# The first group of a fused FFN: order of ScalarE's, VectorE's and SyncE's work at the start

## The chip, the cores and the metric

One core of a Trainium2 chip runs the whole program. Its engines are TensorE (PE), ScalarE (ACT), VectorE (DVE), GpSimd (POOL) and SyncE (SP, which issues the loads). The metric is the device time of one execution in microseconds. TensorE's clock has two levels, 1.2 and 2.4 GHz; the profile gives the granted one as 0.50 and 1.00.

## The reference

Tokens: 2 x 2048 rows of 256 numbers. The program computes a gated FFN with routing, causal attention, and the same FFN again:

```python
x = x + 0.5 * _L0_ffn_ref(_layernorm(x), ...)
x = x + _L0_attn_ref(_layernorm(x), Wq, Wk, Wv, Wo)
x = x + 0.5 * _L0_ffn_ref(_layernorm(x), ...)

# _L0_ffn_ref, the part that the start computes
xln = _ln(x, ln1_w, ln1_b)
att_out = sigmoid(xln @ Wr) * (xln @ Wv) @ Wo
rwkv_state = xln @ Ws                     # used as rwkv_state @ W2
x = x + att_out
h = _ln(x, ln2_w, ln2_b)                  # bids, routing, three experts
```

## The kernel before

Every float32 product is made of three fp32r products: each operand is split in a part hi (the value rounded) and a part lo (value minus hi), and hi*hi, hi*lo, lo*hi are summed. The splits of weights are made once at the start from the raw weights, with the layer norm's weight multiplied in: w_hi by ACT (`split_hi`, L376 and L374), w_lo by DVE (`split_lo`, L384). `early_plan` lists them in order: four for Wr and Wv (RV = 4), then W1, Wo, W3 and the bid columns up to RVS = 10, then two for the product Ws W2 up to EARLY = 12.

The FFN's first part works on 8 groups of 512 rows (NG = 8, four tiles of 128 rows each). For a group g, in order:

- DVE: statistics of the rows (`row_stats`: four bn_stats at L805, four aggregates at L809); POOL: two reciprocal roots of them (`rs1`, L746 to L751, by a power operation at L749)
- ACT: z = normalized rows (`normalize`, L583); PE: z transposed in PSUM (`transpose_z`, L411); ACT: zT_hi (`z_hi`, L619); DVE: zT_lo (`lo`, L824)
- PE: six chains `U(g, n)` of six 512-wide matmuls each (L393): r, v, r, v, then two for the state; a chain needs zT_lo, and from the fourth on the gates that free its bank: n=3 waits for the first sigmoid
- ACT: sigmoid of r (`sig_r`, L632, needs the bias columns); DVE: times v (`gv`, L829); ACT gT_hi (L638), DVE gT_lo (`g_lo`, L835); PE: `Wo(g)`, 24 matmuls of 256
- ACT: y (L598, the doubly normalized rows), s_gate (`sig_s`, L644); DVE: y + Wo's result (L842), then statistics and the second half of the FFN for the groups before

Each engine's queue is written out by hand in a loop over k, in which group k, k-1 and k-2 are in different stages. The waits between engines are semaphores.

At the start there is extra work. PE: `setup_first`, eight one-column products (each 2 matmuls of 128x1; here four columns) of raw_w with the layer norm's bias (L355); `setup_states`, the product of Ws and W2 (L523); `setup_rest`, more one-column products. ACT, in this order: z of group 0, w_hi of Wr and Wv, zT_hi, the other w_hi, the copy of the states' product (L673) and its w_hi, z of group 1, and then the first sigmoid. DVE: statistics of group 0, four w_lo, the bias copy (L932), zT_lo, statistics of group 1, the other w_lo. In later groups row_stats waits for POOL's rs1 of the group before it, ahead of its bn_stats. SP: x0, ln, ident, raw_w (1 MB), raw_w_st (776 KB), x1, five small tables, x2, x3.

Of the kernel before, what the change touches and what calls it, by code (L numbers as in the profile page):

```python
# [62 lines left out]
def build_kernel(nc, x, w256, w_st, k_w, v_w, w_qkv, ln, shares, ident, tri, mask, tok, slot_row, out):  # L63
    with ExitStack() as ctx:
# [258 lines left out]

def setup_sync(sp, b, s, f, xg, given):
    ln, ident, w256, w_st, tri, mask, shares, tok, slot_row = given
    sp.dma_start(b.x[0][:], xg[0]).then_inc(f["x_in"][0], 16)
    sp.dma_start(b.ln[:], ln).then_inc(s.first, 16)
    sp.dma_start(b.ident[:], ident).then_inc(s.first, 16)
    sp.dma_start(b.raw_w[:].rearrange("p m c n -> p (m c n)"), w256).then_inc(s.w, 16)
    sp.dma_start(b.raw_st[:], w_st).then_inc(s.st, 16)  # L330
    sp.dma_start(b.x[1][:], xg[1]).then_inc(f["x_in"][1], 16)
    for to, given in ((b.trif, tri), (b.maskf, mask), (b.shares, shares), (b.tok, tok), (b.slot_row, slot_row)):
        sp.dma_start(to[:], given).then_inc(s.const, 16)
    for g in range(2, X_BUFS):
        sp.dma_start(b.x[g][:], xg[g]).then_inc(f["x_in"][g], 16)
# [40 lines left out]
            act.mul(hi, raw, scale).then_inc(done, 1)  # L376


def split_lo(dve, plan, first, end, ready, done):

    for n in range(first, end):
        raw, scale, hi, lo = plan[n]
        dve.wait_ge(ready, n + 1)
        dve.scalar_tensor_tensor(lo, raw, 1.0 if scale is None else scale, hi.bitcast(F32), ALU.mult,  # L384
                                 ALU.subtract).then_inc(done, 1)

# [28 lines left out]
def ffn_a_tensor(pe, b, f, s, a=None):  # L415

    def U(g, first, end):
        for n, (m, fc) in enumerate(((0, 0), (1, 0), (0, 1), (1, 1), (2, 0), (2, 1))):
            if not first <= n < end:
                continue  # L420
            if n == 0:
                pe.wait_ge(f["zlo"], 2 * g + 2)
                if g >= 2:
                    pe.wait_ge(f["bd"], g - 1)
            if n < 3 and g == 1:
                pe.wait_ge(f["gv"], 2)
# [109 lines left out]

    if s:
        setup_first()
        transpose_z(pe, b, f, 0)
        setup_states()  # L540
    else:
        pe.wait_ge(a["olo"], NB)
        pe.wait_ge(a["exp"], chunk_count(NB))
        pe.wait_ge(a["y"], NB)
    for k in range(NG + 2):
        if k < NG:
            if s and k == 0:
                pe.wait_ge(s.lo, RV)
            U(k, 0, 4)
        if 0 <= k - 2:  # L550
            W3(k - 2)
        if k + 1 < NG:
# [19 lines left out]
            bidT(k - 1)  # L572


def normalize(act, b, f, g, tiles):

    if 0 in tiles:
        act.wait_ge(f["rs1"], g + 1)
# [3 lines left out]
    for t in tiles:  # L582
        last = act.activation(b.z[:, t], b.x[g % X_BUFS][:, t], ACT.Identity, bias=w[:, 6, t:t + 1],  # L583
                              scale=w[:, 4, t:t + 1])
    if GT - 1 in tiles:
        last.then_inc(f["z"], 1)


def ffn_a_scalar(act, b, f, s, a=None):
# [223 lines left out]
def ffn_a_vector(dve, b, f, s, n):  # L813
# [109 lines left out]
    if s:  # L923
# [2 lines left out]
        dve.memset(b.bbias[:], 0.0).then_inc(s.memz, 1)  # L926
        dve.memset(b.ones4[:], 1.0)
        dve.memset(b.cnt[:], 0.0)
        row_stats(dve, b, f, n, 0)
        split_lo(dve, early, 0, RV, s.hi, s.lo)  # L930
        dve.wait_ge(s.bias_mm, 1)
        dve.tensor_copy(b.bias[:, 0:2, :], b.bank(7)[:, 0:2 * CC].rearrange("p (m c) -> p m c", m=2)).then_inc(s.bias, 1)  # L932
        lo(0, f["zhi"], b.zT[0], f["zlo"])
        row_stats(dve, b, f, n, 1)
        split_lo(dve, early, RV, EARLY, s.hi, s.lo)
        dve.wait_ge(s.bias, 1)
    else:
        lo(0, f["zhi"], b.zT[0], f["zlo"])
    for k in range(NG + 2):
# [5 lines left out]
            gv(k, 0)  # L945
        if 0 <= k - 2:
            gates(k - 2)
        if k < NG:
            gv(k, 1)
        if s and k == 0:  # L950
# [3 lines left out]
            dve.tensor_copy(b.bbias[0:BIDS, :], b.bank(5)[0:BIDS, 2 * CC:2 * CC + 1]).then_inc(s.bias, 1)  # L954
            dve.wait_ge(s.const, 16 * 5)
# [3 lines left out]
        if 0 <= k - 2:  # L959
            win(k - 2)  # L960
        if k < NG:
            g_lo(k)
# [872 lines left out]
```

## Time and profile before

| | us |
|---|---|
| median of 3 runs | 1145.62 |
| lowest, highest | 1143.26, 1148.46 |
| the profiled execution | 1147.45 |
| its span | 1145.4 |

TensorE is busy 1002.4 us, VectorE 691.9, ScalarE 566.1, GpSimd 490.9. Times in the rows are from the span's start. A mean granted clock of 0.942 stands over the span. In a timeline a row is: start, time to the end of the last instruction of the row, engine, line, operation, what it writes and reads; behind "idle before" stands how long the engine had stood still, and what released it. PEld is TensorE's weight load, SPq SyncE's queue.

### The profile page before, as it was taken

How to read it: one execution, taken by the hardware profiler on the slowest of the kernel's cores; microseconds unless marked ns; L12 is line 12 of the kernel's file. 1: busy time of each engine (PE TensorE's matmuls, PEld its weight loads, DVE VectorE, ACT ScalarE, POOL GpSimd, SP SyncE). 2: the span in 40 equal slices, each digit the busy share in tenths (PEclk: the TensorE clock that was granted, in tenths of full speed). 3: DMA queues.
4: the chain of work that ended last, by engine and by line, in shares of the span. 5: the costliest groups of instructions: out<-in, count | busy, mean ns of one | idle time of the engine just before them, and what ended most of it. 6: DMA issues, size and time to landing. Idle time of an engine off the chain costs nothing.

```text
span 1145.4 us, 21174 instructions
## 1 busy us (share of the span) xinstructions
PE 1002.4 (88%) x7006; PEld 922.7 (81%) x7007; DVE 691.9 (60%) x1732; ACT 566.1 (49%) x1184; POOL 490.9 (43%) x537
## 2 busy tenths in 40 slices
PE   4899997779999998589998996999998389999994
PEld 4788886779899997578986885788887389999994
DVE  4488878545455553456765676588877355555451
ACT  5567655244454452245554554667663154454450
POOL 3145443435565565741221001254544356566563
PEclk9899998679999999789999998999998699999998
DMA  4021243212211221300121114011211301121120
GB/s 148 1 75 56 75 148 126 78 48 59 77 51 55 58 80 34 97 28 29 37 75 37 38 43 142 16 59 56 88 44 65 111 29 57 57 72 55 55 74 20
DMA packets 50803, 73.13 MB, mean 64 GB/s; under 512 B 5151, under 2 KB 43425, under 8 KB 50081
## 3 DMA queue, kind: packets, MB, share of 16 engines
q1 hardware_dynamic: 42016, 45.75, 13.5%
q0 software_dynamic: 8704, 26.29, 6.1%
q8 instruction: 51, 0.84, 0.3%
q14 instruction: 32, 0.25, 0.1%
HBM read 41.54 MB, written 31.00 MB: 63 GB/s over the span
## 4 chain that ended last, share of the span: by engine, by line
PE 56%; DVE 10%; POOL 3%; DMA 3%; issue 3%; ACT 3%; SPq 0%; DVEq 0%; POOLq 0%; ACTq 0%
PE banks4to L393 27%; PE bank L393 20%; PE banks4to L1456 4%; DVE pT_lo L1696 1%; PE bank L1044 1%; PE bank L1468 1%; DMA slot_z<-routed_rows 1%; POOL attn_x L1778 1%; DVE out_rows L918 1%; ACT pT_hi L1588 1%; DVE zT_lo L824 1%; DVE chunk_max L1686 1%; POOL routed_rows L773 1%; PE bank L481 1%; DVE gT_lo L835 1%
## 5 line engine op out<-in xcount | busy, mean ns | idle before, releaser
L1188 DVE TENSOR_TENSOR relu_squared<-relu 128x512 f32<-128x512 f32 x136 | 157.4, 1172 | 111.3 <-ACT relu L1139 74.5
L1239 POOL TENSOR_TENSOR hr_lo<-relu_squared,hr_hi 128x512 fp32r<-128x512 f32 x136 | 186.4, 1380 | 83.6 <-DVE relu_squared L1188 80.3
L1139 ACT ACTIVATE relu<-bank,slot_k_bias 128x256 f32<-128x256 f32 x204 | 84.8, 467 | 193.2 <-PE bank L393 153.9
L393 PE MATMUL banks4to<-v_hi,hr_hi 128*128 128x256 f32 x544 | 155.4, 286 | 3.6 <-DVE slot_out L1197 2.8
L393 PE MATMUL banks4to<-v_hi,hr_lo 128*128 128x256 f32 x544 | 152.4, 280 | 0.0
L393 PE MATMUL banks4to<-v_lo,hr_hi 128*128 128x256 f32 x544 | 152.3, 280 | 0.0
L393 PE MATMUL bank<-shT_hi,k_hi 128*128 128x256 f32 x408 | 120.4, 295 | 14.8 <-DVE shT_lo L1179 8.5
L773 POOL DMA_INDIRECT routed_rows<-out_rows,row_index x64 | 65.9, 1030 | 152.1 <-DVE row_index L906 137.4
L393 PE MATMUL bank<-shT_lo,k_hi 128*128 128x256 f32 x408 | 118.4, 290 | 0.0
L393 PE MATMUL bank<-shT_hi,k_lo 128*128 128x256 f32 x408 | 118.4, 290 | 0.0
L393 PEld LDWEIGHTS banks4to<-v_hi,hr_hi 128*128 128x128 f32 x544 | 102.4, 188 | 7.4 <-issue 7.2
L393 PEld LDWEIGHTS banks4to<-v_hi,hr_lo 128*128 128x128 f32 x544 | 102.5, 188 | 0.0
L393 PEld LDWEIGHTS banks4to<-v_lo,hr_hi 128*128 128x128 f32 x544 | 102.3, 188 | 0.0
L393 PEld LDWEIGHTS bank<-shT_hi,k_hi 128*128 128x128 f32 x408 | 80.6, 198 | 19.2 <-issue 18.8
L1147 ACT ACTIVATE hr_hi<-relu 128x512 fp32r<-128x512 f32 x136 | 86.1, 633 | 15.2 <-ACT relu L1139 5.5
L393 PEld LDWEIGHTS bank<-shT_hi,k_lo 128*128 128x128 f32 x408 | 80.3, 197 | 0.0
L393 PEld LDWEIGHTS bank<-shT_lo,k_hi 128*128 128x128 f32 x408 | 80.2, 197 | 0.0
L1588 ACT CAST pT_hi<-bank 128x512 fp32r<-128x512 f32 (+1 forms) x72 | 39.1, 564 | 56.5 <-PE bank L1468 56.2
L1579 ACT ACTIVATE p<-banks4to,minus_row_max 128x512 f32<-128x512 f32 (+2 forms) x80 | 49.7, 628 | 31.6 <-DVE minus_row_max L1689 17.6
L1195 DVE COPY token_index<-slot_row 128x2 int32<-128x2 int32 x34 | 5.8, 170 | 95.1 <-PE banks4to L393 95.1
L393 PE MATMUL bank<-zT_hi,w_hi 128*128 128x512 f32 x128 | 55.0, 430 | 8.4 <-ACT r_gate L632 5.8
L1247 POOL DMA_INDIRECT x_after_ffn<-slot_out,token_index x34 | 33.7, 990 | 63.6 <-DVE slot_out L1197 58.4
(246 smaller groups left out, 2995.1 us busy)
## 6 DMA issues: line engine op xcount, KB each, us to landing
slot_row<-routed_rows SPq DMA_DIRECT2D x34, 258.0 KB
slot_z<-routed_rows SPq DMA_DIRECT2D x34, 256.0 KB
x_rows<-in_x SPq DMA_DIRECT2D x8, 512.0 KB, 3.9
attn_x<-x_after_ffn SPq DMA_DIRECT2D x16, 256.0 KB, 2.9
attn_out<-x_after_ffn SPq DMA_DIRECT2D x16, 256.0 KB, 2.7
x_after_attention<-attn_out SPq DMA_DIRECT2D x16, 256.0 KB, 2.1
x_rows<-x_after_attention SPq DMA_DIRECT2D x8, 512.0 KB, 4.0
raw_k<-in_k_w SPq DMA_DIRECT2D x2, 1024.0 KB
```

The source lines that it names most:

```text
L393: mm = pe.matmul(outv, w(pw), m(pm), start=(n_first and k == 0), stop=(n_last and k == 2))
L481: mm = pe.matmul(b.bank(2), b.Wb[:, c], b.hT[p][:, c], start=(c == 0 and p == 0), stop=(c == 1 and p == 1))
L773: pool.indirect_dma_start(routed, bass.IndirectOffsetOnAxis(b.posi[g % 2][:, t:t + 1].bitcast(U32), 0), b.rows[g % 2][:, t, :], None).then ...
L824: dve.tensor_tensor(to[1][:, c], b.bank(c), to[0][:, c].bitcast(F32), ALU.subtract).then_inc(done, 1)
L1139: last = act.activation(b.r[q % 2][:, (h % 2) * SLOT:(h % 2 + 1) * SLOT], b.bank(1 + q)[:, (h % 2) * SLOT:(h % 2 + 1) * SLOT], ACT.Relu, b ...
L1147: act.activation(b.hr[p][0][:, 2 * q:2 * q + 2].rearrange("p h n -> p (h n)"), b.r[q % 2][:, :], ACT.Square).then_inc(f["hrhi"], 1)
L1188: dve.tensor_tensor(b.sq[q % 2][:, :], b.r[q % 2][:, :], b.r[q % 2][:, :], ALU.mult).then_inc(f["sq"], 1)
L1239: pool.tensor_tensor(b.hr[p][1][:, 2 * q:2 * q + 2].rearrange("p h n -> p (h n)"), b.sq[q % 2][:, :], b.hr[p][0][:, 2 * q:2 * q + 2].rearr ...
L1247: pool.indirect_dma_start(dst, bass.IndirectOffsetOnAxis(b.idx[p][:, t:t + 1].bitcast(U32), 0), b.o[p][:, t, :], None, bounds_check=N - 1, ...
L1456: mm = pe.matmul(out[:, at:at + n], b.kq[pw][:, q, 0, t * P:(t + 1) * P], part, start=(k == 0 and i == 0 and not last), stop=(k == 2), ski ...
L1579: act.activation(b.p[s % 2][t][:, c * KEYS:c * KEYS + w], bank(("S", s, t, c))[:, 0:w], ACT.Exp, bias=b.nbias[:, s % 2, t:t + 1], accum_ou ...
L1588: act.copy(b.pT[m % 2][0][:, 0:w], b.bank(m % 2)[:, 0:w]).then_inc(a["pthi"], 1)
```

## The change

In words:

- ACT starts with a sigmoid of a small constant tile. Then z of group 0 with a signal after each tile, zT_hi, the w_hi of plan items 4 to 9, the first sigmoid of group 0, and only then z of group 1. The copy of the states' product and its two w_hi follow the second sigmoid. The four w_hi of Wr and Wv are no longer ACT's.
- DVE makes those four w_hi itself (a multiplication by a per-row scalar), between the statistics of group 1, which now come right behind those of group 0, and zT_lo. Two of the w_lo stand before zT_lo, two after. The two w_lo of the states stand between the two gate products of group 0. Three casts of constants move from k=0 to k=1, and the bias copies behind gT_lo.
- SP loads x0 in halves of two tiles, and x1 ahead of raw_w_st.
- PE makes one column, then transposes z tile by tile, then the other three columns; setup_states moves from before the first chain to behind the third. The chains n=0 and 1 of group 0 wait for their own w_lo.
- `row_stats` waits, in every group, for POOL only behind its bn_stats; ahead of them it waits for its own last aggregate.

```diff
@@ setup_sync
-    sp.dma_start(b.x[0][:], xg[0]).then_inc(f["x_in"][0], 16)
+    front, back = slice(0, GT // 2), slice(GT // 2, GT)
+    sp.dma_start(b.x[0][:, front], xg[0][:, front]).then_inc(s.x0, 16)
+    sp.dma_start(b.x[0][:, back], xg[0][:, back]).then_inc(f["x_in"][0], 16)
     sp.dma_start(b.ln[:], ln).then_inc(s.first, 16)
     sp.dma_start(b.ident[:], ident).then_inc(s.first, 16)
     sp.dma_start(b.raw_w[:].rearrange("p m c n -> p (m c n)"), w256).then_inc(s.w, 16)
+    sp.dma_start(b.x[1][:], xg[1]).then_inc(f["x_in"][1], 16)
     sp.dma_start(b.raw_st[:], w_st).then_inc(s.st, 16)
-    sp.dma_start(b.x[1][:], xg[1]).then_inc(f["x_in"][1], 16)
@@ U, in ffn_a_tensor
+            if s and g == 0 and n < 2:
+                pe.wait_ge(s.lo, 2 * n + 2)
@@ setup_first
-        for m in range(2):
-            for fc in range(CC):
-                mm = column(pe, b.bank(7), m * CC + fc, lambda c: b.raw_w[:, m, c], fc * P, b.ln[:, 1])
+        for n, (fc, m) in enumerate(((0, 0), (0, 1), (1, 0), (1, 1))):
+            mm = column(pe, b.bank(7), m * CC + fc, lambda c: b.raw_w[:, m, c], fc * P, b.ln[:, 1])
+            if n == 0:
+                for t in range(GT):
+                    if t < GT - 1:
+                        pe.wait_ge(s.z0, t + 1)
+                    else:
+                        pe.wait_ge(f["z"], 1)
+                    for c in range(CC):
+                        turned = pe.transpose(b.bank(c)[:, t * P:(t + 1) * P], b.z[:, t, c * P:(c + 1) * P], b.ident[:])
+                        if t == GT - 1:
+                            turned.then_inc(f["T1"], 1)
@@ ffn_a_tensor
         setup_first()
-        transpose_z(pe, b, f, 0)
-        setup_states()
...
         if k < NG:
+            U(k, 0, 3)
             if s and k == 0:
-                pe.wait_ge(s.lo, RV)
-            U(k, 0, 4)
+                setup_states()
+            U(k, 3, 4)
@@ ffn_a_scalar
-        normalize(act, b, f, 0, range(GT))
+        act.wait_ge(s.memz, 3)
+        act.activation(b.sum[:, :], b.half[:, 0, 0:ST], ACT.Sigmoid)
+        normalize(act, b, f, 0, range(GT), s.z0)
+        z_hi(0)
         act.wait_ge(s.first, 32)
         act.wait_ge(s.w, 16)
-        split_hi(act, early, 0, RV, s.hi)
-        z_hi(0)
         act.wait_ge(s.st, 16)
-        act.wait_ge(s.memz, 3)
         split_hi(act, early, RV, RVS, s.hi)
-        act.wait_ge(s.st_mm, 1)
-        act.copy(b.raw_sf[:, :, :], b.bank(6).rearrange("p (c n) -> p c n", c=CC)).then_inc(s.st_raw, 1)
-        act.wait_ge(s.st_raw, 1)
-        split_hi(act, early, RVS, EARLY, s.hi)
+        act.wait_ge(s.bias, 1)
+        sig_r(0, 0)
...
             sig_r(k, 1)
+            if s and k == 0:
+                act.wait_ge(s.st_mm, 1)
+                act.copy(b.raw_sf[:, :, :], b.bank(6).rearrange("p (c n) -> p c n", c=CC)).then_inc(s.st_raw, 1)
+                act.wait_ge(s.st_raw, 1)
+                split_hi(act, early, RVS, EARLY, s.hi)
             g_hi(k, 0)
@@ row_stats
-    dve.wait_ge(f["x_in"][g % X_BUFS], 16 * (g // X_BUFS + 1))
     if g:
-        dve.wait_ge(f["rs1"], g)
+        dve.wait_ge(f["st1"], g)
     for t in range(GT):
+        if t == 0 and front:
+            dve.wait_ge(front, 16)
+        if t == (GT // 2 if front else 0):
+            dve.wait_ge(f["x_in"][g % X_BUFS], 16 * (g // X_BUFS + 1))
         dve.bn_stats(b.st[:, 0, t], b.x[g % X_BUFS][:, t]).then_inc(f["link"], 1)
     links[0] += GT
     dve.wait_ge(f["link"], links[0])
+    if g:
+        dve.wait_ge(f["rs1"], g)
@@ ffn_a_vector
-        row_stats(dve, b, f, n, 0)
-        split_lo(dve, early, 0, RV, s.hi, s.lo)
+        row_stats(dve, b, f, n, 0, s.x0)
+        row_stats(dve, b, f, n, 1)
+        dve.wait_ge(s.first, 32)
+        dve.wait_ge(s.w, 16)
+        for first in (0, 2):
+            for raw, scale, hi, _ in early[first:first + 2]:
+                dve.tensor_scalar(hi, raw, scale, None, ALU.mult).then_inc(s.rv, 1)
+            if first == 0:
+                split_lo(dve, early, 0, 2, s.rv, s.lo)
+        lo(0, f["zhi"], b.zT[0], f["zlo"])
+        split_lo(dve, early, 2, RV, s.rv, s.lo)
         dve.wait_ge(s.bias_mm, 1)
         dve.tensor_copy(b.bias[:, 0:2, :], ...).then_inc(s.bias, 1)
-        lo(0, f["zhi"], b.zT[0], f["zlo"])
-        row_stats(dve, b, f, n, 1)
-        split_lo(dve, early, RV, EARLY, s.hi, s.lo)
+        split_lo(dve, early, RV, RVS, s.hi, s.lo, RV)
...
+        if s and k == 0:
+            split_lo(dve, early, RVS, EARLY, s.hi, s.lo, RV)
         if k < NG:
             gv(k, 1)
```

## Rows read from the trace of the kernel before

**Rows 1.** The page: busy time of each engine, its share of the span, instructions.

```profile
PE 1002.4 (88%) x7006; PEld 922.7 (81%) x7007; DVE 691.9 (60%) x1732; ACT 566.1 (49%) x1184; POOL 490.9 (43%) x537
```

**Rows 2.** Who waited for whom, first 60 us: us in total, times, longest.

```profile
PE bank L393 <- ACT r_gate L632: 5.8, 1, 5.8
```

**Rows 3.** Timeline of ACT and PE around that wait.

```profile
23.07 2.07 ACT L583 ACTIVATE z_rows<-x_rows,rsqrt_work 128x256 f32<-128x256 f32 x4 [4.11 <-POOL rsqrt_work L751]
25.16 1.28 ACT L632 ACT_TABLE_LOAD   x1
26.46 0.69 ACT L632 ACTIVATE r_gate<-bank,bias_cols 128x512 f32<-128x512 f32 x1
27.20 0.79 PE L393 MATMUL bank<-zT_hi,w_hi 128*128 128x512 f32 x1 [5.79 <-ACT r_gate L632]
```

**Rows 4.** Stretches: length, each engine's busy time (instructions), granted clock, DMA share, GB/s.

```profile
26.38:35.10 8.72, 7.90 (x34) 7.18 (x35) 1.50 (x2) 5.49 (x11) 1.53 (x3) 0.50 0.01 2
35.10:40.04 4.94, 4.94 (x13) 3.88 (x14) 3.09 (x9) 1.66 (x3) 0.00 (x0) 0.50 0.00 0
40.04:43.10 3.06, 3.06 (x26) 3.02 (x25) 0.69 (x1) 1.67 (x3) 0.00 (x0) 1.00 0.01 3
```

**Rows 5.** Timeline of PE and its weight loads, from the first column to Wo(0).

```profile
9.32 3.49 PEld L355 LDWEIGHTS banks4to<-ln_cols,raw_w 128*128 128x128 f32 x16 [8.98 <-issue]
12.76 1.95 PE L411 MATMUL bank<-ident_sb,z_rows 128*128 128x128 f32 x8
16.83 0.19 PEld L393 LDWEIGHTS bank<-zT_hi,w_hi 128*128 128x128 f32 x1
35.16 0.77 PE L393 MATMUL bank<-zT_hi,w_hi 128*128 128x512 f32 x1
40.26 0.28 PE L393 MATMUL banks4to<-w_hi,gT_hi 128*128 128x256 f32 x1
```

**Rows 6.** Timeline of DVE, and group 0's z on ACT: statistics, splits, a cast.

```profile
4.78 1.41 DVE L805 BATCH_NORM_STATS2 bn_parts<-x_rows 128x6 f32<-128x256 f32 x4 [3.60 <-DMA x_rows<-in_x]
9.75 2.07 ACT L583 ACTIVATE z_rows<-x_rows,rsqrt_work 128x256 f32<-128x256 f32 x4 [7.72 <-POOL rsqrt_work L751]
12.25 1.68 DVE L384 SCALAR_TENSOR_TENSOR w_lo<-raw_w,ln_cols,w_hi 128x256 fp32r<-128x256 f32 x4 [5.65 <-ACT w_hi L376]
15.96 1.40 DVE L805 BATCH_NORM_STATS2 bn_parts<-x_rows 128x6 f32<-128x256 f32 x4
17.40 0.38 DVE L809 BATCH_NORM_AGGREGATE mean_var<-bn_parts 128x2 f32<-128x6 f32 x4
35.48 0.27 DVE L956 CAST tri_sb<-tri_f 128x256 bf16<-128x256 f32 x1
```

**Rows 7.** Loads of the first 30 us: count, KB, median us from issue to landing.

```profile
raw_w<-in_w SPq DMA_DIRECT2D x1, 1024.0 KB, 7.0
raw_w_st<-in_w_st SPq DMA_DIRECT2D x1, 776.0 KB, 8.4
tri_f<-in_tri SPq DMA_DIRECT2D x1, 128.0 KB, 8.8
```

**Rows 8.** Timeline of PE: setup_rest at half speed, a later group's transposes at full.

```profile
14.49 2.71 PE L523 MATMUL banks4to<-raw_w_st 128*128 128x256 f32 x8
31.41 1.82 PEld L355 LDWEIGHTS banks4to<-ln_cols,raw_w 128*128 128x128 f32 x8
48.72 1.04 PE L411 MATMUL bank<-ident_sb,z_rows 128*128 128x128 f32 x8
```

**Rows 9.** Timeline of DVE in k=1, where the casts go.

```profile
54.03 1.29 DVE L824 TENSOR_TENSOR zT_lo<-bank,zT_hi 128x512 fp32r<-128x512 f32 x2 [1.76 <-ACT zT_hi L619]
```

**Rows 10.** Timeline of POOL: the same operation beside DVE's splits and alone.

```profile
18.26 1.58 POOL L747 TENSOR_SCALAR rsqrt_work<-mean_var 128x4 f32<-128x4 f32 x1
25.33 0.23 POOL L747 TENSOR_SCALAR rsqrt_work<-mean_var 128x4 f32<-128x4 f32 x1
```

**Rows 11.** Stretches as in rows 4, around the one-column products on raw_k.

```profile
217.50:231.20 13.70, 11.47 (x55) 11.38 (x54) 5.97 (x12) 0.00 (x0) 7.25 (x6) 0.50 0.40 149
```

More of the change, by code:

```diff
@@ L192, in build_kernel @@
         s.barrier, s.fence = sem("phase_done"), sem("fence")
+        s.x0, s.z0, s.rv = sem("x0_front_loaded"), sem("z0_tiles"), sem("weights_rv_hi")
         s.first, s.const, s.w, s.st = sem("ln_ident_loaded"), sem("const_loaded"), sem("w256_loaded"), sem("w_st_loaded")
@@ L376, in split_hi, with split_lo @@
             act.mul(hi, raw, scale).then_inc(done, 1)
-def split_lo(dve, plan, first, end, ready, done):
+def split_lo(dve, plan, first, end, ready, done, earlier=0):
     for n in range(first, end):
         raw, scale, hi, lo = plan[n]
-        dve.wait_ge(ready, n + 1)
+        dve.wait_ge(ready, n + 1 - earlier)
         dve.scalar_tensor_tensor(lo, raw, 1.0 if scale is None else scale, hi.bitcast(F32), ALU.mult,
@@ L572, in ffn_a_tensor, with normalize @@
             bidT(k - 1)
-def normalize(act, b, f, g, tiles):
+def normalize(act, b, f, g, tiles, each=None):
     if 0 in tiles:
@@ L584, in normalize @@
                               scale=w[:, 4, t:t + 1])
+        if each and t < GT - 1:
+            last.then_inc(each, 1)
     if GT - 1 in tiles:
@@ L686, in ffn_a_scalar @@
             split_hi(act, late, 0, K_ITEMS, s.k_hi)
-        if k < NG:
-            if s and k == 0:
-                act.wait_ge(s.bias, 1)
+        if k < NG and not (s and k == 0):
             sig_r(k, 0)
@@ L796, in ffn_a_gpsimd, with row_stats @@
                                 pad, None).then_inc(f["pad"], 16)
-def row_stats(dve, b, f, links, g):
-    dve.wait_ge(f["x_in"][g % X_BUFS], 16 * (g // X_BUFS + 1))
+def row_stats(dve, b, f, links, g, front=None):
     if g:
-        dve.wait_ge(f["rs1"], g)
+        dve.wait_ge(f["st1"], g)
     for t in range(GT):
+        if t == 0 and front:
+            dve.wait_ge(front, 16)
+        if t == (GT // 2 if front else 0):
+            dve.wait_ge(f["x_in"][g % X_BUFS], 16 * (g // X_BUFS + 1))
         dve.bn_stats(b.st[:, 0, t], b.x[g % X_BUFS][:, t]).then_inc(f["link"], 1)
@@ L947, in ffn_a_vector @@
             gates(k - 2)
+        if s and k == 0:
+            split_lo(dve, early, RVS, EARLY, s.hi, s.lo, RV)
         if k < NG:
             gv(k, 1)
+        if 0 <= k - 2:
+            win(k - 2)
+        if k < NG:
+            g_lo(k)
         if s and k == 0:
@@ L954, in ffn_a_vector @@
             dve.tensor_copy(b.bbias[0:BIDS, :], b.bank(5)[0:BIDS, 2 * CC:2 * CC + 1]).then_inc(s.bias, 1)
+        if s and k == 1:
             dve.wait_ge(s.const, 16 * 5)
@@ L958, in ffn_a_vector @@
             dve.tensor_copy(b.identb[:], b.ident[:])
[L959 to L962, printed above, removed]
         if 0 <= k - 2:
```

## The prediction

> **What bounds the kernel now.** I read the busy table first: TensorE (PE) is busy for 88% of the span, VectorE (DVE) 60%, ScalarE (ACT) 49% [rows 1], so what shortens PE's standing still can shorten the whole. The edit lies almost wholly in the first 40 us, so the question is what PE waits for there. The waits of the first 60 us name one long wait after the start: PE 5.8 us for the sigmoid r_gate on ACT [rows 2]. The timeline shows why. PE's first three product chains end at 21.4 (27.20 less the 5.79 idle before it). ACT could take the sigmoid then, but group 1's normalization (four z_rows) stands ahead of it and waits for GpSimd's (POOL's) reciprocal root, done just before 23.07; after it comes a 1.28 us table load; the sigmoid starts at 26.46, PE at 27.20 [rows 3]. Then the table of stretches: after this idle time the granted clock reads 0.50 from 26.38 to 40.04, and 1.00 afterwards [rows 4]. At 0.50 (1.2 GHz) 12 product matmuls take 35.16 to 40.26, 0.43 us each; the first 18, from 16.86 to 21.4, took 0.25 each, 0.23 once under way (2.4 GHz) [rows 3, 5]. So the wait costs twice: 5.8 us, and half speed for the 13 us behind it.
>
> From group 1 on (Wo(0) begins at 40.26) nothing is tied to an absolute time: x2 and x3 were issued by 9.7 us, and the later work waits for earlier work only. I therefore take the shift of Wo(0) as the shift of the end.
>
> **The start, part by part.** Half of x0 saves at most 0.7 us of its statistics (half of 1.41, begun at 4.78 when the whole had landed), less an issue of 0.43 to 0.49 that now stands before each later load [rows 6, 7]; I take 0.5: group 0's z starts near 9.25 instead of 9.75. raw_w landed at 2.25 + 7.0 = 9.25 and w_st at 2.73 + 8.4 = 11.1; w_st's 776 KB thus took 1.9 us behind raw_w [rows 7]. x1's 512 KB, moved ahead of w_st, take by the same rate 1.3: it lands between 10.5 and 11.1 (the extra issue hidden or not), I take 10.8; if the order brings nothing it is 12.5, as for tri behind it (3.68 + 8.8). Everything on DVE (all splits, zT_lo, the bias copy that the first sigmoid needs) is queued behind this wait for x1. w_st in turn lands 1.3 later, near 12.4; ACT comes to it at 13.0.
>
> PE does one column (0.9), then transposes each tile as ACT ends it (0.52 apart); the last are through near 11.8 instead of 14.7. ACT's two zT_hi copies end near 13.0. This gain is hidden, because DVE now has more ahead of zT_lo: statistics of group 1 (1.82, rows 15.96 to 17.78) from 10.8 to 12.6; four multiplications w_hi; two w_lo (0.42 each); then the two zT_lo (1.3). Of the multiplications no row exists: a cast of the same shape took 0.27, the two-input form 0.48, spaced 0.42 [rows 6]. I take 0.35 between them, 1.4 in all. Sum: 12.6 + 1.4 + 0.85 + 0.15 for gaps + 1.3 = 16.3, and U(0) starts at 16.4 (bounds 15.9 to 18.1) against 16.86. Before, setup_states (2.4 us) held it; that work now sits behind the third chain.
> The Trainium skill (VectorE: DVE Perf Modes, section The perf-mode tier table) lets an fp32 multiplication by a scalar inside SBUF run two elements a cycle; by that the four would cost about 0.3 us less than I take, as an estimate. No row of before shows such an instruction of this size.
>
> **The clock at the start.** The clock column reads 1.00 up to 26.38, but durations speak first: weight loads of the same shape took 0.33 us in the columns at 9.3, and 0.19 from 16.8 [rows 5]. The rise came at the end of setup_states, with PE unbroken since 9.35 and transposes and 256-wide products since 12.76. After, PE is idle from about 14.5 to 16.4 and the states are gone, so U(0) starts at half speed. The two rises on record came 3.4 us after the transposes began (12.76 to about 16.14) and 4.9 us after the unbroken products of 35.16 began [rows 4, 5, 8]. I take 4.9: rise at 21.3; each us later costs 0.45. Eighteen matmuls then end at 22.9 instead of 21.4: a **loss of 1.5**.
>
> **The wait that goes.** ACT's sigmoid now follows the first chain (19.0 to 19.7), its table load has moved to 0.7 us where ACT idles until 9.25, and group 1's z (2.07) follows to 21.8. The second sigmoid ends at 23.6. PE does not stand: **gain 5.8**. In its place come setup_states, 1.5 (weight loads of 0.19) to 2.7 (of 0.33), I take 1.6: **loss 1.6**. Queued behind it is U's fourth chain, which needs the first sigmoid alone.
>
> **Work that gets its speed back.** The fourth chain 2.7, transposes 1.9, setup_rest 3.7 (31.41 to 35.16), fifth and sixth chains 5.1: 13.06 us from 27.20 to 40.26 [rows 3, 5, 8]. At full clock: 1.4, 1.04 (48.72), about 2.0 (weight loads limit it, 0.33 to 0.19), 2.8: 7.2. **Gain 5.8.** Sum: 5.8 + 5.8 - 1.5 - 1.6 = **8.5 us**; Wo(0) at 31.7.
>
> **Who is late next.** ACT: copy of the states' product 24.6, two w_hi (0.91) to 26.05, first gT_hi to 26.7; DVE's w_lo of these stand ahead of the second gate product (to 27.35), so gT_hi ends at 28.0, y (2.07) at 30.1, zT_hi at 31.1, s_gate, half a z, s_gate: 33.6. U(1) needs that and PE comes to it at 34.5: 0.9 us of slack. DVE's three casts, 0.7 us, move to k=1, where 1.76 us of idle time before zT_lo at 54.03 takes them [rows 9]. The statistics' wait for POOL moves behind bn_stats: among DVE's waits from 60 us on none of bn_stats for POOL stands, so that is worth nothing later.
>
> **The reference point.** The profiled run took 1147.45 us (span 1145.4), 1.8 above the median of 1145.62. Less 8.5 gives 1139.0 by the run that carries the sum and 1137.1 by the median. I say 1138. A change has to pass 0.5%, 5.7 us (below 1139.9), to be told from none.
>
> **Rivals.**
> - *DVE or POOL late in the start (0.10).* From the end of DVE's statistics to ACT's z POOL's work took 3.1 in group 0 (6.6 to 9.75) but 5.3 in group 1 (17.78 to 23.07), while DVE's two-input splits ran; L747 took 1.58 instead of 0.23 [rows 3, 6, 10]. From 12.6 it ends at 15.7, 17.9, or at 22.4 if all five of its operations stretch by the 1.35 of L747. Up to 21.7 it is hidden (20.8, and ACT's 0.9); beyond that 0.7 is lost. With x1 at 12.5 another 1.7. It would give 8.5 - 2.4 = 6.1: 1139.5 by the median, 1141.4 by the profiled run, 1140.4 between.
> The Trainium skill (SBUF — State Buffer, section Who interferes with whom) says a VectorE instruction with two SBUF inputs blocks a GpSimd one that reads SBUF; by that rule the trace agrees (1.58 against 0.23).
> - *The clock falls again (0.15).* During the one-column products on raw_k the reading stays 0.50 from 217.5 to 231.2, with PE busy 11.5 of 13.7 us [rows 11]. In setup_rest there are 2 us of them. If the clock falls behind them, chains five and six cost 5.1 instead of 2.8: gain 6.2, 1139.4 to 1141.3, 1140.3 between.
> - *Full speed only after setup_rest (0.05), the slower side.* Broken up by transposes and columns, 7.9 us of work from 27.2 did not bring the clock back [rows 8]. If the first chains don't either, they end at 24.1, then 2.7 and 13.06: Wo(0) at 39.9; at half speed Wo's 24 matmuls cost 5.1 instead of 2.8 and U(1)'s 24 of 512 4.7 more. It decides where the rise comes later than about 41: slower by 2 to 6.6, 1147.6 to 1152.
> - *The profile shows more than the median holds (0.12).* If the clock's fall in the wait is an accident of this run, other runs of before reach Wo(0) at 27.2 + 7.2 = 34.4 and only 2.7 are won: 1142.9. Against it: PE did nothing for 5.8 us, and its cause, the order of ACT's queue, is there in every run.
>
> **How the numbers follow.** Forecast 0.58, its own range 1136 to 1140.5 (start 15.9 to 18.1, rise 3.4 to 7.9 us in, the latter a stretch that brought none, states 1.5 to 2.7). With the rivals up to 1142.9 but not the slow case: 1135 to 1143. Faster by over 0.5%: 0.52 of the forecast, 0.06 of DVE or POOL, 0.06 of the clock's fall: 0.64. Within: the rest of those (0.19), the accident (0.12): 0.31. Slower: 0.05.
>
> **What would show it.** After: no ACT_TABLE_LOAD behind the first; PE's first product of w and zT near 16.4, with 0.43 between the first ones and 0.23 later; no idle time over 1 us on PE between it and Wo; states' products behind 18 matmuls; Wo(0) near 31.7 instead of 40.26; U(1) directly behind it. Wrong if PE waits before the sixth chain or U(1) (then ACT's queue is late), if U(0) starts past 18, or if Wo(0) came 8 us earlier and the end did not.

## The result

| | us |
|---|---|
| before, median of 9 runs | 1145.62 |
| changed, median of 9 runs (lowest, highest) | 1139.6 (1135.88, 1142.89) |
| ratio, 95% interval | 0.9948, 0.9932 to 0.9964 |
| profiled execution, before and changed | 1147.45 and 1138.35 |
| their spans | 1145.4 and 1136.4 |

The change wins 6.0 us by the medians and 9.1 by the profiled executions. The prediction was 1138 with a range of 1135 to 1143.

The timeline of TensorE (PE) in the changed kernel: the first product, the first matmul after the step of the clock, the states' product, the fourth chain, transposes, Wo(0) and U(1). It answers to [rows 3, 5, 8].

```profile
15.81 0.77 PE L396 MATMUL bank<-zT_hi,w_hi 128*128 128x512 f32 x1 [1.21 <-DVE zT_lo L845]
21.04 0.39 PE L396 MATMUL banks4to<-zT_hi,w_hi 128*128 128x512 f32 x1
22.44 1.89 PE L537 MATMUL banks4to<-raw_w_st 128*128 128x256 f32 x8
23.98 0.58 PE L396 MATMUL bank<-zT_hi,w_hi 128*128 128x512 f32 x1
25.57 1.03 PE L414 MATMUL bank<-ident_sb,z_rows 128*128 128x128 f32 x8
31.30 0.28 PE L396 MATMUL banks4to<-w_hi,gT_hi 128*128 128x256 f32 x1
34.12 0.40 PE L396 MATMUL bank<-zT_hi,w_hi 128*128 128x512 f32 x1
```

Wo(0), the first product with Wo, begins at 31.30 instead of 40.26, U(1), the first product of group 1, at 34.12 instead of 43.11: 9.0 us earlier. The spans are 9.0 us apart too: behind U(1) both executions took 1102.3 us. That this part came out equal is luck, as the comparison of the profiles below shows. The interval of the medians, 4.1 to 7.8 us, doesn't hold the 9.0.

The stretches of the changed kernel (length; busy time of PE, weight loads, DVE, ACT, POOL; granted clock; DMA share; GB/s), against [rows 4]:

```profile
12.00:15.80 3.80, 2.60 (x14) 2.53 (x13) 3.77 (x14) 3.29 (x8) 2.77 (x6) 1.00 0.87 268
15.80:20.99 5.19, 5.17 (x12) 4.13 (x13) 4.69 (x17) 2.18 (x5) 0.63 (x3) 1.00 0.00 1
20.99:31.30 10.31, 10.31 (x61) 8.87 (x60) 4.89 (x10) 7.36 (x15) 2.31 (x5) 1.00 0.01 2
```

From 15.80 on PE is busy without a gap. 12 matmuls fill 15.80 to 20.99, 0.43 us each: half speed, although the clock column reads 1.00 there (it holds no record before the first step). From 20.99 they come every 0.23.

ScalarE (ACT), VectorE (DVE) and GpSimd (POOL) in the same kernel, against [rows 3, 6, 10]:

```profile
0.74 1.28 ACT L680 ACT_TABLE_LOAD   x1 [0.74 <-PEq L1856]
3.66 1.49 DVE L824 BATCH_NORM_STATS2 bn_parts<-x_rows 128x6 f32<-128x256 f32 x4 [2.48 <-DMA x_rows<-in_x]
8.71 2.07 ACT L596 ACTIVATE z_rows<-x_rows,rsqrt_work 128x256 f32<-128x256 f32 x4 [6.46 <-POOL rsqrt_work L767]
10.84 1.41 DVE L824 BATCH_NORM_STATS2 bn_parts<-x_rows 128x6 f32<-128x256 f32 x4 [5.28 <-DMA x_rows<-in_x]
12.57 0.58 DVE L956 TENSOR_SCALAR w_hi<-raw_w,ln_cols 128x256 fp32r<-128x256 f32 x2
13.01 0.24 POOL L763 TENSOR_SCALAR rsqrt_work<-mean_var 128x4 f32<-128x4 f32 x1
14.39 1.28 DVE L845 TENSOR_TENSOR zT_lo<-bank,zT_hi 128x512 fp32r<-128x512 f32 x2
15.54 0.57 POOL L767 TENSOR_TENSOR rsqrt_work<-rsqrt_work 128x4 f32<-128x4 f32 x2
18.81 0.69 ACT L647 ACTIVATE r_gate<-bank,bias_cols 128x512 f32<-128x512 f32 x1 [3.45 <-PE bank L396]
19.40 2.06 ACT L596 ACTIVATE z_rows<-x_rows,rsqrt_work 128x256 f32<-128x256 f32 x4
```

DVE stands until x1 lands at 10.84 and has no gap from there to the first product: it sets U(0). POOL's result for group 1 is there at 16.1 instead of 23.07. ACT waits 3.45 us for the first chain; before, it waited 4.11 us for POOL at this place [rows 3].

### The profile page after: what moved, and what is told of

Its sections match the earlier page's. It is cut to its first block, busy times and chain, and to the rows that moved or that the text cites. A ratio compares the mean times of both kernels' runs of the same rounds, so it can differ in the third digit from the quotient of the medians.

```text
span 1136.4 us, 21189 instructions
## 1 busy us (share of the span) xinstructions
PE 997.6 (88%) x7006; PEld 919.3 (81%) x7007; DVE 694.1 (61%) x1736; ACT 563.1 (50%) x1180; POOL 489.0 (43%) x537
## 4 chain that ended last, share of the span: by engine, by line
PE 57%; DVE 9%; POOL 3%; issue 3%; DMA 3%; ACT 3%; SPq 0%; DVEq 0%; POOLq 0%; ACTq 0%
PE banks4to L396 28%; PE bank L396 20%; PE banks4to L1487 4%; DVE pT_lo L1727 1%; PE bank L1499 1%; PE bank L1075 1%; POOL attn_x L1809 1%; DMA slot_z<-routed_rows 1%; DVE out_rows L939 1%; ACT pT_hi L1619 1%; DVE zT_lo L845 1%; DVE chunk_max L1717 1%; POOL routed_rows L789 1%; PE bank L486 1%; DVE gT_lo L856 1%
## 5 line engine op out<-in xcount | busy, mean ns | idle before, releaser
L396 PEld LDWEIGHTS bank<-shT_hi,k_hi 128*128 128x128 f32 x408 | 80.5, 197 | 18.9 <-issue 18.5
L1727 DVE TENSOR_TENSOR pT_lo<-bank,pT_hi 128x512 fp32r<-128x512 f32 (+1 forms) x72 | 46.2, 658 | 22.6 <-ACT pT_hi L1619 22.2
```

The costliest lines, as they stand in the source:

```text
L396: mm = pe.matmul(outv, w(pw), m(pm), start=(n_first and k == 0), stop=(n_last and k == 2))
L1727: dve.tensor_tensor(b.pT[m % 2][1][:, 0:w], b.bank(m % 2)[:, 0:w], b.pT[m % 2][0][:, 0:w].bitcast(F32), ALU.subtract).then_inc(a["ptlo"], 1)
```

## The experiments

Two marks are read in each kernel's timeline: U(0), the first product of w and zT, and U(1), which in the changed kernel follows Wo(0) by 2.8 us. Medians stand beside those of the kernel before timed in the same session (1146.56 for before_again and e1 to e3, 1146.07 for after_again and e4 to e6, 1147.36 for e7 to e9, 1145.99 for before_third).

| kernel | U(0) | U(1) | clock steps to 45 us | median (runs) | ratio, 95% interval |
|---|---|---|---|---|---|
| before | 16.86 | 43.11 | up 16.1, down 26.4, up 40.0 | 1145.62 (9) | |
| before_again | 16.64 | 42.92 | up 15.7, down 26.0, up 39.6 | 1147.05 (10) | 0.9998, 0.9972 to 1.0024 |
| before_third | 16.76 | 38.66 | up 17.5, down 24.3, up 31.1 | 1145.46 (10) | 1.0003, 0.9976 to 1.0029 |
| changed | 15.81 | 34.12 | up 21.0 | 1139.6 (9) | 0.9948, 0.9932 to 0.9964 |
| after_again | 15.27 | 33.95 | up 21.3 | 1139.54 (10) | 0.9941, 0.9916 to 0.9965 |
| e1_order_only | 16.99 | 36.64 | up 16.8, down 27.0, up 33.8 | 1141.49 (10) | 0.9961, 0.9934 to 0.9987 |
| e2_fill_wait | 16.72 | 36.89 | up 16.3 | 1140.55 (10) | 0.9952, 0.9925 to 0.9979 |
| e3_sigmoid_behind | 14.73 | 32.40 | up 18.5 | 1138.48 (10) | 0.9943, 0.9918 to 0.9967 |
| e4_x1_behind | 17.95 | 36.49 | up 23.6 | 1141.05 (10) | 0.9954, 0.9930 to 0.9978 |
| e5_rv_on_act | 14.55 | 32.85 | up 19.7 | 1134.84 (5) | 0.9900, 0.9867 to 0.9934 |
| e6_no_early_table | 15.26 | 33.31 | up 19.9 | 1141.51 (1) | |
| e7_states_first | 16.91 | 32.81 | up 16.8, down 27.0, up 30.4 | 1141.72 (1) | |
| e8_kept_warm | 15.00 | 30.96 | up 4.5 | 1132.34 (4) | 0.9890, 0.9833 to 0.9948 |
| e9_both | 14.35 | 30.24 | up 4.9, down 42.4 | 1134.84 (7) | 0.9895, 0.9857 to 0.9933 |

Executions of one kernel spread by 6 to 12 us (lowest to highest), so parts worth one or two microseconds are read from the marks and not from the medians.

### Is the profile of before typical?

**before_again**, no edit.

> The kernel before once more, with a second profile. Profile against profile the change won 9.1 us (1147.45 to 1138.35), median against median 6.0 (1145.62 to 1139.6). Theory A (the clock's changes fall differently in each execution, and this moves runs of one kernel by 2 to 5 us): Wo(0) stands within 2 us of 40.3 again, the wait of 5.8 us and the fall to 0.50 behind it are there again, and the span follows the mean granted clock. Rival B (the fall of the clock in the wait is an accident of the first profile): the stretch 27 to 40 reads 1.00 and Wo(0) begins near 34.4.

U(1) at 42.92, the wait and the fall behind it as before: theory A. Its span was 1151.6 all the same, with a mean granted clock of 0.935 instead of 0.942 (it fell again at 56.7): behind U(1) it took 6.4 us longer.

**after_again**, no edit.

> The changed kernel once more, timed beside the kernel before. In the first session the medians stood 6.0 us apart and the profiled executions 9.1, with the start shifted by 9.0 (U(1) at 34.12 against 43.11). Theory A (all 9.0 us arrive at the end, and the rest is noise of the clock, which moves single executions by several us): ratio nearer to 0.993 (8 us) than to 0.995. Rival B (about 3 us are given back in unprofiled executions, the clock falling more often later on): ratio again 0.9945 to 0.9955.

The ratio of 0.9941 lies between the two expectations, and its interval holds both. U(1) stood at 33.95: the start of the changed kernel repeats. Both pairs of profiles give 9.0 for the start, the medians 6.0 and 6.5. Hence a third profile of the kernel before.

**before_third**, no edit.

> The kernel before, a third profile. The start is 9.0 us longer than in the changed kernel in two profiles of each, and yet the medians stand only 6.0 and 6.5 us apart. Both profiles of before had nearly the same record of the clock: up at 16.1 and 15.7, down at 26.4 and 26.0, up at 40.0 and 39.6. Theory A (the steps of the clock lie differently in other executions, and where the fourth chain and the transposes from 27.2 to 31 fall together before a step, the clock rises near 31 and the start is 3 to 5 us shorter): a profile whose first rise is not near 16 shows the second near 28 to 33 and U(1) at 37 to 40. Rival B (the start is the same in every execution, and the missing 2 to 3 us go later on): U(1) at 42.9 to 43.2 whatever the clock's record.

Two lines of PE, the fourth chain's start and U(1), and the stretches of this execution, as above:

```profile
26.41 0.79 PE L393 MATMUL bank<-zT_hi,w_hi 128*128 128x512 f32 x1 [4.76 <-ACT r_gate L632]
38.66 0.40 PE L393 MATMUL bank<-zT_hi,w_hi 128*128 128x512 f32 x1
17.49:24.32 6.83, 4.16 (x18) 3.01 (x16) 4.31 (x15) 3.40 (x7) 4.56 (x6) 1.00 0.00 0
24.32:31.14 6.82, 4.73 (x17) 4.04 (x17) 1.50 (x2) 4.12 (x7) 2.61 (x6) 0.50 0.00 0
31.14:38.66 7.52, 7.52 (x55) 6.92 (x56) 3.78 (x10) 5.87 (x12) 0.00 (x0) 1.00 0.01 3
```

Theory A. The clock fell in the same wait, but at 24.3, and rose at 31.1, in the midst of the work in which it stayed low until 40 in the other two. The half speed cost the fourth chain and the transposes only, and U(1) came at 38.66. The start of before is thus 38.7 to 43.1 long from one execution to the next, that of the changed kernel 34.0 or 34.1 in two: a gain of 4.5 to 9.2, into which the 6.0 and 6.5 of the medians fall. How often each case occurs three profiles can't say, so that this is why the medians show less is argued and not shown.

The part behind U(1) differs more than the starts do. It took 1102.3 us in both first profiles, but 1098.3 to 1108.7 over the 14 profiles of all kernels here, and it is longest where the clock stood longest at half speed: 138 us behind U(1) in before_again, 106 in e8_kept_warm, the shortest. The parts of the edit that lie there (the wait in `row_stats`, the three casts) were not tried alone. The five kernels with the old code took 1101.7 to 1108.7 there, the nine with the new 1098.3 to 1107.8: an effect of a few us of these parts can't be seen or excluded.

### What in the wait cost how much?

**e2_fill_wait**: the wait of before stays, PE is given work in it.

```diff
             if n == 3:
+                if s and g == 0:
+                    for _ in range(24):
+                        pe.matmul(b.bank(5), b.W[0][:, 0, 0, 0:P], b.zT[0][0][:, 0], start=True, stop=True)
                 pe.wait_ge(f["sigr"], 2 * g + 1)
```

> The kernel before, with 24 products of 512 that nobody reads, issued by TensorE in the wait for the first sigmoid; the wait itself stays. It measures the clock's part alone. Theory A (half of the gain was the clock): the granted clock reads 1.00 through, PE resumes at 27.2 as before and needs 7.2 us instead of 13.06 to Wo(0), which begins near 34.4: 5.8 us less by the profile. Rival B (at full clock another engine, ScalarE's y and zT_hi in the same stretch, becomes the bound): Wo(0) near 34.4 but U(1) later than directly behind it, the end only 3 to 5 us earlier.

```profile
21.12 5.76 PE L435 MATMUL banks4to<-zT_hi,w_hi 128*128 128x512 f32 x24
21.10:26.90 5.80, 5.80 (x26) 4.39 (x24) 1.87 (x9) 4.18 (x7) 3.48 (x7) 1.00 0.00 0
26.90:34.07 7.17, 7.17 (x47) 6.26 (x47) 4.12 (x11) 5.75 (x12) 0.65 (x3) 1.00 0.01 2
```

Rows of the timeline and of the stretches. The 24 products fill the wait (the fourth chain resumes at 26.83), the clock stays up, and the same work takes 7.2 us to Wo(0) instead of 13.06: 5.8 us are the clock's, and U(1) follows Wo(0) directly, so theory A. By the medians 6.0 us (2.4 to 8.6 by the interval), as much as the whole change, although not one wait was removed.

**e1_order_only**: in the kernel before, the first sigmoid goes ahead of group 1's z.

```diff
+        act.wait_ge(s.bias, 1)
+        sig_r(0, 0)
     else:
         z_hi(0)
     normalize(act, b, f, 1, range(GT))
...
-        if k < NG:
-            if s and k == 0:
-                act.wait_ge(s.bias, 1)
-            sig_r(k, 0)
+        if k < NG and not (s and k == 0):
+            sig_r(k, 0)
```

> The kernel before, with one edit: the first sigmoid goes ahead of group 1's z on ScalarE. Theory A (the order of that queue is the whole cause): the table load and the sigmoid end near 21.0, the fourth chain follows the third without a wait, PE then waits some 2.4 us for group 1's z (its POOL input is done at 23.04 as before), too short to lose the clock, and Wo(0) begins at 31.1: the gain is that of the whole change, 9 us by the profile, 6 by the medians. Rival B (the other parts, splits on VectorE and earlier x1, carry part of it): the wait moves to z's transposes, the clock falls in it, Wo(0) near 34 to 36, gain 3 to 5 by the profile.

```profile
22.75 2.07 ACT L583 ACTIVATE z_rows<-x_rows,rsqrt_work 128x256 f32<-128x256 f32 x4 [1.84 <-POOL rsqrt_work L751]
24.87 1.09 PE L411 MATMUL bank<-ident_sb,z_rows 128*128 128x128 f32 x8 [1.94 <-ACT z_rows L583]
24.87:27.00 2.13, 2.13 (x21) 2.09 (x22) 1.18 (x2) 1.87 (x4) 1.92 (x4) 1.00 0.00 0
27.00:33.80 6.80, 6.80 (x21) 5.64 (x22) 3.09 (x9) 4.41 (x9) 0.59 (x3) 0.50 0.01 2
```

Theory A had the wait right (1.94 us, for z) and the clock wrong; rival B describes it. PE's wait, transposes and one-column products follow each other from 23 to 27, then the clock falls, and the fifth and sixth chains run at 0.43. U(1) at 36.64: the order of one queue won 6.5 of the 9.0, counted from the first profile of before (2.0 from the third), and 5.1 by the medians. That the other 2.5 come with an earlier z of group 1 is read from this wait; e7 below, which has z early and the states' product in its old place, agrees with 32.81.

**e3_sigmoid_behind**: the changed kernel with the sigmoid behind group 1's z again.

```diff
-        act.wait_ge(s.bias, 1)
-        sig_r(0, 0)
     else:
         z_hi(0)
     normalize(act, b, f, 1, range(GT))
+    if s:
+        act.wait_ge(s.bias, 1)
+        sig_r(0, 0)
```

> The changed kernel, with the edit that gives it its name undone: the first sigmoid stands behind group 1's z again; all else as changed. Theory A (with x1 and its statistics early, POOL's result is there at 16.1 and z fits into ScalarE's idle time from 15.4 to 18.8): z from 16.2 to 18.3, sigmoid at 18.8 as in the changed kernel, Wo(0) at 31.3, no difference beyond noise. Rival B (POOL or the order of queues makes z late): the sigmoid ends after 21.5, PE waits, and some of the 9 us come back.

```profile
15.06 2.08 ACT L596 ACTIVATE z_rows<-x_rows,rsqrt_work 128x256 f32<-128x256 f32 x4 [0.56 <-POOL rsqrt_work L768]
17.72 0.69 ACT L647 ACTIVATE r_gate<-bank,bias_cols 128x512 f32<-128x512 f32 x1 [0.58 <-PE bank L396]
```

Theory A. z fits in front of the sigmoid, which still starts when the first chain ends. Once x1 and the statistics of group 1 are early, the sigmoid's new place is worth nothing. Either this or the sigmoid's place takes the 5.8 us wait away; the sigmoid's place alone leaves the 1.94 us of e1. (This execution got raw_w at 8.30, 1.2 us earlier than the changed kernel's, and its clock rose at 18.5, which is its 1.7 us at U(1).)

### The parts of the start

**e4_x1_behind**: the changed kernel with x1 behind w_st.

```diff
-    sp.dma_start(b.x[1][:], xg[1]).then_inc(f["x_in"][1], 16)
     sp.dma_start(b.raw_st[:], w_st).then_inc(s.st, 16)
+    sp.dma_start(b.x[1][:], xg[1]).then_inc(f["x_in"][1], 16)
```

> The changed kernel, x1 loaded behind w_st as before. Theory A (everything on VectorE waits for x1, nothing hides it): bn_stats of group 1 starts at 12.4 instead of 10.84, U(0) at 17.4 instead of 15.8, Wo(0) at 32.5 to 32.9 instead of 31.30, 1.2 to 1.6 us lost. Rival B (there was slack on another engine): U(0) within 0.5 of 15.8.

```profile
12.98 1.40 DVE L824 BATCH_NORM_STATS2 bn_parts<-x_rows 128x6 f32<-128x256 f32 x4 [7.51 <-DMA x_rows<-in_x]
17.95 0.77 PE L396 MATMUL bank<-zT_hi,w_hi 128*128 128x512 f32 x1 [3.25 <-DVE zT_lo L845]
```

Theory A: x1 2.1 us later is U(0) 2.1 and U(1) 2.4 us later, more than the 1.2 to 1.6 expected, since x1 came at 12.98 and not at 12.4. Every microsecond of x1 counts in full, because of the order in which DVE takes it: from the start of group 1's statistics to U(0) it is 4.97 to 4.99 us in the changed kernel's two profiles and in e3, e4, e6 and e8, wherever x1 landed.

**e5_rv_on_act**: the changed kernel with the four w_hi back on ACT.

```diff
         normalize(act, b, f, 0, range(GT), s.z0)
-        z_hi(0)
         act.wait_ge(s.first, 32)
         act.wait_ge(s.w, 16)
+        split_hi(act, early, 0, RV, s.rv)
+        z_hi(0)
@@ ffn_a_vector
-            for raw, scale, hi, _ in early[first:first + 2]:
-                dve.tensor_scalar(hi, raw, scale, None, ALU.mult).then_inc(s.rv, 1)
```

> The changed kernel, with the four w_hi of Wr and Wv made by ScalarE again, between z and zT_hi. Theory A (VectorE is the bound of the start, and ScalarE has 3.45 us of idle time before its sigmoid, so this part of the change costs time): zT_lo ends 0.7 earlier, U(0) near 15.0 instead of 15.81, Wo(0) near 30.6 instead of 31.30, the sigmoid still at the end of the first chain. Rival B (ScalarE becomes the bound: zT_hi 1.7 later, at 13.8 to 14.8, as before the change): zT_lo and U(0) no earlier or up to 0.7 later than in the changed kernel.

```profile
10.62 1.41 DVE L825 BATCH_NORM_STATS2 bn_parts<-x_rows 128x6 f32<-128x256 f32 x4 [5.13 <-DMA x_rows<-in_x]
12.21 1.05 ACT L634 CAST zT_hi<-bank 128x512 fp32r<-128x512 f32 x2
13.12 1.28 DVE L846 TENSOR_TENSOR zT_lo<-bank,zT_hi 128x512 fp32r<-128x512 f32 x2
14.55 0.77 PE L396 MATMUL bank<-zT_hi,w_hi 128*128 128x512 f32 x1 [0.16 <-DVE zT_lo L846]
```

Theory A. zT_lo starts at 13.12 instead of 14.39, U(0) and U(1) come 1.27 us earlier. Of this 0.22 are x1's, whose statistics began at 10.62 instead of 10.84; from there to U(0) it is 3.93 us instead of 4.97. One of the parts of the change thus costs 1.0 us: it moved work from the engine with idle time to the one that sets the start. The median, 1134.84 of 5 runs, lies lower than that explains; why is not shown, and the marks carry the verdict.

**e6_no_early_table**: the changed kernel without the sigmoid at ACT's start.

> The changed kernel without the small sigmoid at ScalarE's start. Theory A (the table load is placed right behind the instruction before the sigmoid and runs in ScalarE's idle time, 15.4 to 16.7): a second load of 1.28 there, the first sigmoid at 18.8, Wo(0) at 31.3: this part is worth nothing. Rival B (the load waits with the sigmoid for the first chain): load at 18.8, sigmoid at 20.1; group 1's z ends at 22.8 and the second sigmoid at 23.6, 0.3 later, which the states' products still hide.

```profile
8.62 1.28 ACT L596 ACT_TABLE_LOAD   x1 [8.62 <-POOL rsqrt_work L766]
18.24 1.28 ACT L647 ACT_TABLE_LOAD   x1 [2.40 <-PE bank L396]
```

Rival B, and more: both loads stand behind the wait of the instruction they belong to, the first one too, which makes group 0's z 1.3 us later. Neither shows in U(0) (15.26, against 15.27 in after_again) nor in U(1), which is 0.64 earlier, with the clock's step at 19.9 instead of 21.3. This part is worth nothing while DVE sets the start.

**e7_states_first**: the changed kernel with `setup_states()` behind `setup_first()` instead of behind the third chain.

> The changed kernel, with the product of the states back ahead of the first chain. Theory A (the chains start when zT_lo is there, and the states' product behind the columns, from 14.6 to 17.2 at half speed, is in their way): U(0) at 17.3 instead of 15.3 to 15.8, Wo(0) about 0.5 to 1 later, since the 1.9 us of it behind the third chain go and the clock rises earlier. Rival B (without a gap on TensorE the clock rises near 16, as in the kernel before, and gives all back): the 18 matmuls at 0.23 each, Wo(0) at 29.5 to 30.5, earlier than in the changed kernel.

```profile
13.86 3.41 PE L537 MATMUL banks4to<-raw_w_st 128*128 128x256 f32 x8
25.54 0.47 PE L396 MATMUL bank<-zT_hi,w_hi 128*128 128x512 f32 x1
20.40:27.00 6.60, 6.60 (x45) 5.81 (x44) 3.48 (x8) 5.78 (x13) 2.37 (x5) 1.00 0.02 4
27.00:30.40 3.40, 3.40 (x11) 2.79 (x10) 1.29 (x2) 3.40 (x7) 0.00 (x0) 0.50 0.00 0
```

Rival B. U(0) at 16.91, but the clock is up at 16.8 as in the kernel before, the chains run at full speed, Wo(0) begins at 29.58, and U(1) comes at 32.81, 1.1 to 1.3 us earlier than in the changed kernel. It would be near 31.1 (an estimate: half of the 3.4 us at half speed less) if the clock had not fallen at 27.0, with PE busy all the time: transposes and one-column products to 25.54, then the fifth chain. Moving the states away cost the warm start that they gave. This rests on the marks of one profile; the kernel was timed once, and that time (1141.72) shows no gain.

**e8_kept_warm**: the changed kernel with products nobody reads in PE's idle time.

```diff
     def setup_first():
+        pe.wait_ge(s.memz, 3)
+        idle_products(44)
         pe.wait_ge(s.first, 32)
...
+                    if t < GT - 1:
+                        idle_products(2)
         mm.then_inc(s.bias_mm, 1)
+        pe.wait_ge(f["zhi"], 1)
+        for _ in range(20):
+            pe.matmul(b.bank(5)[:, 0:C], b.zT[0][0][:, 0, 0:P], b.zT[0][0][:, 0, 0:C], start=True, stop=True)
```

`idle_products(n)` issues n matmuls of the zeroed bid weights into bank 5.

> The changed kernel, with products that nobody reads on TensorE from 1.3 to 9.4 us (44 of 256 columns), 2 behind each of the first three transposed tiles and 20 behind the columns. It measures what the half speed of the first chains costs. Theory A (the term of 1.5 to 2.6 us in the sum is the clock's alone): weight loads of 0.19 from the columns on, 18 matmuls of U at 0.23, third chain ended at 20.0 instead of 22.4, Wo(0) at 28.9 instead of 31.3, 2.4 us less. Rival B (the clock falls again in the columns and transposes from 9.4 to 14): the 20 products take 4.3 us instead of 2.3, U(0) starts at 17 or later, Wo(0) no earlier than 31.3.

```profile
1.23 6.96 PE L517 MATMUL banks4to<-w_bid 128*128 128x256 f32 x44 [1.23 <-DVE bid_bias L958]
8.63 0.58 PE L358 MATMUL banks4to<-ln_cols,raw_w 128*128 128x1 f32 x4 [0.44 <-DMA raw_w<-in_w]
15.00 0.47 PE L396 MATMUL bank<-zT_hi,w_hi 128*128 128x512 f32 x1
28.14 0.28 PE L396 MATMUL banks4to<-w_hi,gT_hi 128*128 128x256 f32 x1
```

Theory A. The clock is up from 4.5, a column's four matmuls take 0.58 instead of 0.99, and U(0) to Wo(0) take 13.1 us instead of 15.5 (changed) and 15.9 (after_again): 2.4 to 2.7 us are the cold start. U(1) at 30.96 is 3.2 us before the changed kernel's; 0.8 of that is an earlier x1 in this execution (U(0) at 15.00), so the edit's own part is 2.4.

**e9_both**: the edits of e5 and e8 together, with 12 products at the end instead of 20.

> Both at once: w_hi of Wr and Wv on ScalarE as in e5, and TensorE kept at work as in e8 (12 products behind the columns instead of 20). Theory A (both gains add): U(0) at 14.5, Wo(0) at 27.6, 3.7 us less than the changed kernel, 12 less than before, by the medians 1133 to 1136. Rival B (ScalarE, now with more ahead of zT_hi and a sigmoid due at 16, becomes the bound): Wo(0) no earlier than 28.9.

U(0) at 14.35, Wo(0) at 27.39, U(1) at 30.24: theory A, 3.9 us before the changed kernel, 12.9 before the kernel before (8.4 against its third profile). As in e8, 0.8 of the 3.9 is an earlier x1 (10.04 instead of 10.84), and 3.1 are the edits'. Its median is 1134.84, with a ratio of 0.9895; e8's is 1132.34, with a wider interval that holds it. Both lie below both kernels; which of the two is faster these runs don't say. In e9's profile the clock fell once more, at 42.4, in PE's 2.9 us wait ahead of group 0's second transposes. That wait, for zT_lo, stands in all 14 profiles, and in five of them the clock fell in it or up to 1.4 us behind it (56.7 in before_again, 51.6 in before_third, 50.4 in e2, 45.8 in e3). No run here tries to remove or fill it.

## Why the prediction was right, and where it was off

| step | forecast | measured in the changed kernel |
|---|---|---|
| z of group 0 starts | 9.25 | 8.71 |
| x1 lands | 10.8 | 10.84 |
| statistics of group 1 end | 12.6 | 12.66 |
| four w_hi on DVE | 1.4 us | 1.0 us (0.50 + 0.52, start to start) |
| U(0) | 16.4 | 15.81 |
| the clock rises | 21.3 | 21.0 |
| third chain ends | 22.9 | 22.44 |
| states' product | 1.6 us | 1.5 us |
| fourth chain to Wo(0) | 7.2 us | 7.3 us |
| Wo(0) | 31.7 | 31.30 |
| sum | 8.5 us | 9.0 us |

- **The wait that goes: right.** PE has no gap from 15.80 to U(1). The gain of 5.8 came in full, and so did that of the clock behind it; e2 puts the latter at 5.8. The parts that the prediction lists for these 13.06 us add up to 13.4, because the transposes' 1.9 run into setup_rest; the total was read by itself and is right.
- **The start is DVE's: right, and cheaper than taken.** With x0 in halves its statistics began 1.1 us earlier (3.66 against 4.78) and group 0's z 1.0 and not 0.5, but that stayed hidden as forecast. By the Trainium skill's rule on fp32 multiplications (VectorE: DVE Perf Modes, section The perf-mode tier table) the four would have cost 0.3 us less than I took; from start to start they cost 0.4 less (0.50 and 0.52 for two, 0.30 for one from start to end), and the trace agrees. I did not see that e5's arrangement, ACT making the four, was open and 1.0 us better.
- **The cold start: right in kind, 1.0 instead of 1.5.** The rise came 5.2 us after the first product. e8 gives what it costs in full, 2.4 to 2.7, most of which the kernel before did not pay: it had the states' product in front (e7).
- **Who is late next: right.** ACT's second s_gate ended at 32.80, PE came to U(1) at 34.12.
- **POOL late: did not happen.** From the statistics' end at 12.66 POOL took 3.5 us and not 5.3. L763, L747 in the kernel before, took 0.24 instead of 1.58; it began beside DVE's multiplications and ended beside a two-input split. The next one, wholly beside that split, took 0.29 instead of the 0.96 of the kernel before. Which of DVE's instructions stretch POOL's, and when, these runs don't separate.
- **The clock falls again: not in the changed kernel's two profiles, but in e1's and e7's,** both times at 27.0. In e1 it fell amid the one-column products, with a wait of 1.94 us before the transposes; in e7 there was no wait, and 1.5 us of the fifth chain stood between the columns and the fall. e8 has the same sequence 0.3 us earlier and no fall. So the fall that the rival feared exists, the cause that it gave is not shown, and the chance of 0.15 was not too high.
- **The reference point: the step that was off.** The shift of 9.0 at U(1) is that of the profiled executions as well (1147.45 - 9.0 = 1138.4; 1138.35 measured), but that is luck: behind U(1) executions differ by up to 10 us. Against medians it is 6.0 to 6.5. The rival "the profile shows more than the median holds" was put as all or nothing, a clock that does not fall. The profiles of before show something between: the clock falls in all three, but comes back at 40.0, 39.6 or 31.1. Its term (13.06 us of work at half speed) should have carried a range of its own, 2 to 6 us of gain instead of 5.8 (in before_third this work took 9.4 us instead of 13.06, and 7.2 at full speed). I had taken a middle between both references, 1138, which lies 1.6 below the measured median; the range held it.

## What to carry to other kernels

A short wait of TensorE can cost as much again behind it, in work at half speed; count the work up to the next rise, and give that term a range, since the rise comes at another place in each execution. When a queue's order is repaired in two ways at once, test each alone: here one of the two was enough to remove the long wait. Compare marks from the landing of the load on which they depend: it moved by over 1 us between executions, as much as the parts that were to be measured. Move work to the engine that waits, not away from it, and look at what a moved piece of work did besides its result: the states' product, in front of the chains, had warmed TensorE's clock for them.

## What the runs showed of the hardware

- Products that nobody reads, issued in idle time, gave TensorE back 5.8 us (e2) and 2.4 to 2.7 us at the start (e8). U(0) came 0.15 us behind zT_lo's end in e8 and 0.26 in e9, against 0.14 in the changed kernel: they delayed it by 0.1 us at most.
- PE was busy in 6.60 of the 6.60 us before the clock fell at 27.0 in e7: 512-wide products to 22.70, transposes and one-column products to 25.54, then six more 512-wide products. In e8 the same sequence, 0.3 us earlier, brought no fall.
- The first rise came 5.2 and 6.0 us after the first product in the two profiles of the changed kernel, 3.8 in e3, and 3.2 us after the first idle product in e8.
- x1's landing differs between executions: 10.84 and 10.29 in the changed kernel, 9.74 in e3, in the same place of the queue. U(0) followed it by 4.97 to 4.99 us each time. raw_w landed at 9.35, 9.33 and 8.55 in three profiles of before.
- A table load stands with its instruction behind that instruction's wait: at 8.62 and 18.24 in e6, and at 0.74, ahead of the small sigmoid, in the changed kernel.
